# Second feed-forward pass: three fp32 down-projection tiles in place of an f16 part and a rest for two of them

## What is computed

```python
def _quantize_activations_groupwise(x):      # 5 groups of 6 images, the last 2 images give 0
    for g in range(NUM_GROUPS):
        ag = x[g * gs:(g + 1) * gs]
        gamma = jnp.max(jnp.abs(ag))
        xq = xq.at[g * gs:(g + 1) * gs].set(jnp.clip(ag * QB / (gamma + EPS), -QB + EPS, QB - EPS))
    return xq

def _bitlinear(x, W, b):
    Wb = _binarize_weights_groupwise(W)      # -1, 0 or 1
    y = jnp.einsum('btc,oc->bto', x, Wb) + b
    return _quantize_activations_groupwise(y)
h = _bitlinear(x, W1, b1)                    # 96 -> 384
h = jax.nn.gelu(h, approximate=False)
out = _bitlinear(h, W2, b2)                  # 384 -> 96
```

## Time and profile before

| | |
|---|---|
| median of 3 runs | 942.24 us (942.08 to 942.28) |
| profiled execution, first to last instruction | 940.3 us |
| TensorE busy in that span | 850.6 us, 90% |
| VectorE busy | 709.4 us, 75% |
| ScalarE busy | 473.9 us, 50% |
| GpSimd busy | 249.0 us, 26% |
| second pass | about 750 to 924 us of the span |

### The profile page before, as it was taken

One profiled execution on the slowest core, in us unless ns is written; L12 is line 12 of the kernel. 1 busy time (PEld: TensorE's weight loads), 2 busy tenths in 40 slices (PEclk: granted clock), 3 DMA queues, 4 the chain that ended last, 5 costly groups with the idle time before them and its releaser, 6 DMA issues.

```text
span 940.3 us, 18317 instructions
## 1 busy us (share of the span) xinstructions
PE 850.6 (90%) x6053; PEld 683.1 (73%) x6053; DVE 709.4 (75%) x2091; ACT 473.9 (50%) x614; POOL 249.0 (26%) x201
## 2 busy tenths in 40 slices
PE   1799929999999999999999999999999799888882
PEld 1799916788888888888888888888888655444441
DVE  4678982577777777777778777777777558999998
ACT  2244131354545454545445454545454398788981
POOL 1002610223222322322232223222322002434542
PEclk9999995899999999999999999999999999999996
DMA  9910000011001100100010001001110010363334
GB/s 214 232 35 0 1 0 14 14 30 51 26 26 38 39 26 26 51 26 26 26 51 26 26 26 51 26 26 29 47 32 20 14 39 14 103 180 97 108 103 141
DMA packets 19950, 48.35 MB, mean 51 GB/s; under 512 B 4622, under 2 KB 4818, under 8 KB 19922
## 3 DMA queue, kind: packets, MB, share of 16 engines
q1 hardware_dynamic: 17008, 46.97, 18.3%
q10 hardware_dynamic: 2914, 1.03, 0.6%
HBM read 29.33 MB, written 18.67 MB: 51 GB/s over the span
## 4 chain that ended last, share of the span: by engine, by line
PE 69%; DVE 10%; issue 8%; DMA 5%; POOL 5%; ACTq 1%; ACT 1%; SPq 0%; DVEq 0%; POOLq 0%
PE slot L799 17%; PE slot L780 10%; PE slot L709 9%; PE slot L842 8%; POOL xs L511 5%; PE slot L929 5%; PE slot L727 4%; PE slot L900 4%; DMA xs<-out 3%; PE slot L806 3%; PE slot L809 3%; PE slot L794 3%; DVE W2last L1163 2%; DMA projb<-in_L_attn_proj_b 1%; ACTq L521 1%
## 5 line engine op out<-in xcount | busy, mean ns | idle before, releaser
L799 PE MATMUL slot<-w2s,hT 128*112 128x96 f32 x1344 | 166.7, 273 | 0.0
L1234 DVE TENSOR_SCALAR xh<-t,ln_mv,ln_rs 112x96 f32<-112x96 f32 x434 | 109.3, 325 | 60.0 <-POOL ln_rs L483 60.0
L799 PEld LDWEIGHTS slot<-w2s,hT 128*112 128x112 f32 x1344 | 145.3, 181 | 11.0 <-issue 0.5
L608 ACT ACTIVATE hT<-slot,b1c,w_unit 128x784 f32<-128x784 f32 x96 | 95.9, 1005 | 105.2 <-PE slot L780 105.2
L488 POOL TENSOR_TENSOR xn_lo<-xn,xn_hi 96x784 f16<-96x784 f32 x32 | 53.4, 1670 | 272.0 <-ACT xn_hi L597 272.0
L615 ACT ACTIVATE stage<-slot,minus_one 112x768 f32<-112x768 f32 x64 | 52.5, 821 | 119.4 <-PE slot L842 119.3
L511 POOL TENSOR_TENSOR xs<-xs,xn 96x784 f32<-96x784 f32 x24 | 64.1, 2670 | 127.8 <-DVE xn L1377 93.5
L483 POOL TENSOR_TENSOR ln_rs<-ln_ve,pow_half 112x7 f32<-112x7 f32 x62 | 91.8, 1481 | 4.8
L662 ACT ACTIVATE hT<-slot,s 128x784 f32<-128x784 f32 x90 | 81.0, 926 | 20.4 <-DVE stage L1347 14.4
L806 PE MATMUL slot<-big,W1b 99*128 (+1 forms) x360 | 90.2, 331 | 0.0
L809 PE MATMUL slot<-big,W1b 96*128 (+1 forms) x360 | 89.9, 330 | 0.0
(11 more groups left out here) (178 smaller groups left out, 1504.7 us busy)
## 6 DMA issues: line engine op xcount, KB each, us to landing
big<-in_x SPq DMA_DIRECT2D x8, 1176.0 KB, 11.4
xs<-in_x SPq DMA_DIRECT2D x32, 294.0 KB, 3.1
out<-t2T SPq DMA_DIRECT2D x32, 294.0 KB, 3.3
xs<-out SPq DMA_DIRECT2D x24, 294.0 KB, 3.2
out<-xs SPq DMA_DIRECT2D x24, 294.0 KB, 2.7
big<-out SPq DMA_DIRECT2D x1, 1764.0 KB, 10.5
out<-big SPq DMA_DIRECT2D x6, 294.0 KB, 2.6
w_raw<-in_L_conv_w ACTq DMA_DIRECT2D x2, 144.0 KB
```

What stands on the lines that cost most here:

```text
L608: nc.scalar.activation(hT[:, t, :].rearrange("p (a n) -> p a n", a=2), halves((0, one, 2)[t], P), ACT.Relu, scale=w1_unit[:, t:t + 1], bia ...
L799: ins = mm(o[:, j, :], hT[:, t, j * TOK:(j + 1) * TOK], w2s[:, v, t, :], start=False, stop=t == TILES - 1, skip_group_check=True)
L1234: ins = V.tensor_scalar(dst[:, j, :], src[:, j, :], ln_mv[n][:, j, 0:1], ln_rs[n][:, j:j + 1], ALU.subtract, ALU.mult)
```

## The change

All three inner tiles are kept as clipped fp32 in `hc`, three tiles for each of two images in turn, in the memory that held the parts and rests. ScalarE's casts (`gelu_hi`) and their semaphore `hi_parts` go. VectorE's `split` becomes one clip for each tile, and takes over the wait until the buffer of two images earlier is free. `W2b` is fp32, `W2last` and its copy go, and TensorE does 6 fp32 matmuls per image in place of 8 with f16 and 2 with fp32.

```diff
-        W2b = sb("W2b", [P, TILES, C], BF16)
-        W2last = sb("W2last", [P, C])
+        W2b = sb("W2b", [P, TILES, C])
...
-        stage16 = stage[:, :].bitcast(F16)
-        SPLIT = TILES - 1
-        part = SPLIT * HW
-        per_r = 2 * part + 2 * HW
-        h_hi, h_lo = ([stage16[:, r * per_r + n * part:r * per_r + (n + 1) * part].rearrange(
-            "p (t n) -> p t n", t=SPLIT) for r in range(2)] for n in range(2))
-
-        h_last = [stage16[:, r * per_r + 2 * part:(r + 1) * per_r].bitcast(F32) for r in range(2)]
+        hc = [stage[:, r * TILES * HW:(r + 1) * TILES * HW].rearrange("p (t n) -> p t n", t=TILES) for r in range(2)]
...
-            def gelu_hi(b, t, r):
-                wait_apart(act, gelu_ready, 3 * b + t + 1, act_passed)
-                if t == 0:
-                    wait_count(act, y2_ready, b - 1)
-                    if not isinstance(b, int):
-                        act.sem_inc(act_passed, 1)
-                nc.scalar.copy(h_hi[r][:, t, :], gel[:, t, :]).then_inc(hi_parts, 1)
...
-                    gelu_hi(b, 0, r)
                     gelu_tile(g, b, 2)
-                    gelu_hi(b, 1, r)
...
-                for t in range(SPLIT):
+                for t in range(TILES):
                     pe.wait_ge(parts_ready, 3 * b + t + 1)
-                    for part, src in enumerate((h_hi[r], h_lo[r])):
-                        for h in range(2):
-                            mm(S[3][0:C, h, 0:HALF], W2b[:, t, :], src[:, t, h * HALF:(h + 1) * HALF],
-                               start=t == 0 and part == 0, stop=False, skip_group_check=True)
-                pe.wait_ge(parts_ready, 3 * b + TILES)
-                for h in range(2):
-                    ins = mm(S[3][0:C, h, 0:HALF], W2last[:, :], h_last[r][:, h * HALF:(h + 1) * HALF],
-                             start=False, stop=True, skip_group_check=True)
+                    for h in range(2):
+                        ins = mm(S[3][0:C, h, 0:HALF], W2b[:, t, :], hc[r][:, t, h * HALF:(h + 1) * HALF],
+                                 start=t == 0, stop=t == TILES - 1, skip_group_check=True)
                 ins.then_inc(y2_ready, 1)
...
-            V.tensor_copy(W2last[:, :], W2b[:, TILES - 1, :])
...
             def split(m, r):
                 b = 2 * m + r
-                for t in range(SPLIT):
-                    dve.wait_ge(hi_parts, SPLIT * b + t + 1)
-                    V.scalar_tensor_tensor(h_lo[r][:, t, :], gel[:, t, :], Q_CLIP, h_hi[r][:, t, :],
-                                           ALU.min, ALU.subtract).then_inc(parts_ready, 1)
-                dve.wait_ge(gelu_ready, 3 * b + 3)
-                V.tensor_scalar(h_last[r][:, :], gel[:, 2, :], Q_CLIP, None, ALU.min).then_inc(parts_ready, 1)
+                wait_count(dve, y2_ready, b - 1)
+                for t in range(TILES):
+                    dve.wait_ge(gelu_ready, 3 * b + t + 1)
+                    V.tensor_scalar(hc[r][:, t, :], gel[:, t, :], Q_CLIP, None, ALU.min).then_inc(parts_ready, 1)
```

More of the change, by code:

```diff
@@ L361, in build @@
         qc_ready = sem("qc_ready")
-        hi_parts = sem("hi_parts")
         o_ready = sem("o_ready")
```

## The result

The changed kernel takes 956.77 us (median of 4 runs, 955.51 to 957.44), the kernel before on the same chip 942.26 (942.08 to 943.22). The ratio is 1.0148, with a 95% interval of 1.0133 to 1.0162. It is slower by 14.5 us. The prediction was 955.1, in a range of 952.3 to 959.5. The profiled execution spans 954.8 us against 940.3.

The account below looks back on a forecast made before the run. TensorE was to become the second pass's bound at 5.97 us per image. +13.7 for the pass, -0.6 tail and -0.2 setup make +12.9 on 942.24, so 955.1 us, range 952.3 to 959.5.

Parts of the forecast that it names:

- TensorE becomes the bound: Second feed-forward pass: tiles 0 and 1 go from 0.66 to 1.32 us each, making TensorE's period 5.97 against 5.54.
- The sum of the pass: Second pass: 30 down-projections, 28 up-projections, four boundaries and holds end it at 936.9 against 923.23, +13.7 us.
- The boundaries: Four group boundaries in the second pass: TensorE's transposing and broadcasting costs 0.98 us each, 3.9 in all.
- The holds: Behind the four boundaries: VectorE's clips held by GpSimd's additions come late, 0.3 us each, 1.2 in all.
- The start: Up to the first down-projection: 0.3 us earlier as a TensorE wait goes, and 0.2 from the setup.
- The setup: Setup: removing the weight tile's copy gains only 0.2 us, as GpSimd's memset holds the next cast to 109.16 instead.
- Rival B: Setup: the cast behind the removed copy is not held, 10.9 to 12.4 us earlier, 943 to 944; chance 0.04.
- The tail: End of the pass: the last absmax no longer waits behind a held clip, 0.6 us less.
- Rival A: Later groups: VectorE's 3.82 and a GpSimd add of 2.17 bound them, 5 to 10 us more, 960 to 965; chance 0.12.
- One sign: Second pass: among the signs of a right forecast, VectorE was to idle for the GELUs; no size given.
- What bounds the kernel before: Second pass before: no engine bounds all of it; ScalarE's 5.34 us per image is nearly the period of 5.54.
- rival C: Second pass: TensorE is not the bound if an fp32 tile costs under 1.18 us; 15 saved, 927; chance 0.01.

Follow-up runs that it names:

- experiment 2: The changed kernel with ScalarE's two casts per image kept, into a spare tile that nothing reads: 956.70 us.
- experiment 5: The changed kernel without the down-projection matmuls of tile 1, its share of the result left out: 923.76 us.
- experiment 6: The changed kernel with GpSimd's addition for each finished image cut from 784 columns to 2: 955.52 us.
- Experiment 3: The kernel before with GpSimd's memset of ones moved earlier, to where GpSimd idles: 931.92 us, ratio 0.9877.
- experiment 1: The changed kernel with tile 0 back as f16 part and rest, tiles 1 and 2 clipped fp32: 945.20 us, ratio 1.0020 to the kernel before.
- experiment 12: The kernel before with the ones written early, additions on VectorE, four residual buffers instead of two and some loops written out: 911.71 us, ratio 0.9672.
- experiment 9: The changed kernel with the residual addition joined to VectorE's second clip and none on GpSimd: 955.19 us, ratio 1.0142 to the kernel before.

## Why the prediction held, point by point

**TensorE becomes the bound, and each tile costs 0.66 more.** Right, and shown from both sides: 1.68 us more of casts on ScalarE changed nothing (experiment 2), 1.32 less on TensorE changed much (experiment 5). The period was 5.95 against 5.97.

**The sum of the pass.** 180.2 was predicted and 180.7 measured, partly by luck. The boundaries cost 0.83 each and not 0.98, 0.6 less in all, and 30 down-projections of 3.95 and 28 up-projections of 2.00 are 0.6 less than counted. One term was missing. The last down-projection has no up-projection in front, so it waits for the eviction of the image before:

```profile
931.61 1.48 PE L941 MATMUL slot<-stage,W2b 128*96 128x392 f32 x4
934.26 1.23 PE L941 MATMUL slot<-stage,W2b 128*96 128x392 f32 x3 [1.17 <-ACT big L658]
```

From 931.61 + 4 x 0.33 = 932.9 to 934.26 are 1.3 us that my count of up- and down-projections doesn't contain. The holds that I put at 1.2 are 1.3 by experiment 6, and they lie where the prediction had them: the down-projection of the next image behind each of the four boundaries takes 0.13, 0.35, 0.34 and 0.42 longer than 3.95, and in experiment 6 it does not.

**The start.** The time from the span's start to the first down-projection was predicted 0.5 shorter (0.3 for a wait, 0.2 in the setup) and came 0.6 longer. With the 0.5 of the pass this makes up, to a tenth, the 1.6 between 953.2 and the span of 954.8. The 0.3 was too much in any case: the 0.40 in the earlier trace rows is idle time of the weight loads, and the matmul in question started 0.17 late, at 756.31 instead of 755.81 + 0.33. That wait did go. That only 0.6 separate the two starts is luck. In the kernel before and in the changed one:

```profile
130.00:200.00 70.00, 61.05 (x371) 45.94 (x370) 36.40 (x136) 24.40 (x32) 11.74 (x11) 0.78 0.06 18
...
726.00:757.00 31.00, 25.86 (x181) 20.90 (x180) 14.81 (x41) 12.07 (x19) 1.68 (x2) 0.89 0.08 21
...
734.11 1.52 PE L929 MATMUL slot<-R,xh1T 97*112 97x96 f32 x14
```

```profile
130.00:200.00 70.00, 60.87 (x406) 47.67 (x403) 38.94 (x151) 26.42 (x34) 13.44 (x13) 0.85 0.06 18
...
729.94 1.52 PE L910 MATMUL slot<-R,xh1T 97*112 97x96 f32 x14
```

The changed kernel began the first pass 0.3 later (142.49 against 142.19). At its beginning it had the higher granted clock, 0.85 against 0.78, and at the same matmuls near its end it was 4.2 ahead, 729.94 against 734.11. From there to the first down-projection it had the lower clock (0.68 from 726 to 757.6, last section) and took 27.7 where the kernel before took 22.9. Two differences of 4.5 and 4.8 us, neither of them a term of mine, nearly cancelled.

**The setup.** Right in its mechanism: the hold moved to the next cast, to 109.55. The 0.2 us of gain don't show at the start of the first pass. Rival B's price was right too. Experiment 3 frees the setup by taking away the memset instead of the copy, and gains 11.3, against 10.9 to 12.4.

**The tail.** The last absmax follows its eviction at once, 939.52 after 938.58 + 0.91, and the tail is 0.5 shorter; 0.6 was predicted.

**Rival A** is out as the bound of the later groups: in the changed kernel, the boundaries aside, all their images but one of each group take 5.95 to 6.03. That one takes 6.08 to 6.37, and in experiment 5 it still takes 6.0, with TensorE's work cut to 4.63: there the rival's reckoning is close.

**One sign did not come.** VectorE was to idle for the GELUs. In the pass it waits 2.9 us for them, and 32.3 us for the evictions ahead of its absmax.

**What bounds the kernel before: this reading was wrong, though the sum didn't rest on it.** I gave ScalarE 5.34 us per image from the durations of its records. They overlap. In the timeline of the kernel before, at a busy place:

```profile
773.73 0.96 ACT L662 ACTIVATE hT<-slot,s 128x784 f32<-128x784 f32 x1
774.54 0.89 ACT L671 CAST stage<-hT 128x784 f16<-128x784 f32 x1
775.27 0.96 ACT L675 ACTIVATE big<-slot,fb2c 96x784 f32 x1
776.08 1.76 ACT L662 ACTIVATE hT<-slot,s 128x784 f32<-128x784 f32 x2
```

From start to start a GELU and an eviction cost 0.81, a cast 0.73: 4 x 0.81 + 2 x 0.73 = 4.70 per image. The first group of the kernel before, in which GpSimd adds nothing, already runs at this pace:

```profile
771.67 1.52 PE L961 MATMUL slot<-stage,W2b 128*96 128x392 f16 x8
...
776.37 1.52 PE L961 MATMUL slot<-stage,W2b 128*96 128x392 f16 x8
```

So ScalarE, 27.66 of 28.00 busy, or TensorE with its 4.65 bounds there, and neither explains 5.54. Most of what made 5.54 of it was the hold of VectorE by GpSimd, worth 21.0 us of the pass. The same mistake stands in rival C: a TensorE need below 5.54 was not enough to win, as experiment 1 showed with 5.29.

So the change did remove a stall of some 21 us, but with more work of TensorE, 39.6, in its place: 166.2 - 21.0 + 39.6 = 184.8 would be the sum if no other slack took part, and 180.7 was measured. Where hardly anybody else is in the way (experiment 12's form against experiment 9's), three fp32 tiles cost 179.4 - 148.0 = 31.4 us more in the pass.

## What to carry to other kernels

A change that relieves two engines and loads the third is settled by the third's start-to-start times alone, if these come out above the present period. Before one acts on a period that no engine's work explains, look for clips and casts from SBUF to SBUF on VectorE with durations several times their median, and see what GpSimd does beside them: here one such addition per image and one memset in the setup cost 21 and 11 us, and joining the addition to a VectorE instruction, moving the memset, and loading further ahead took 31 us off the kernel before, to which the change added 14.5. And what an instruction is held by matters more than its length: the weight tile's copy, 15.69 us long, was removed, and the next cast took its place.

## What the runs showed of the hardware

A GpSimd addition of 1.84 us alone is recorded with up to 3.89 where VectorE's instructions on two SBUF inputs run beside it, and VectorE's clip of 0.56 with 2.1 to 2.25 where the addition came first. That the one which comes later waits to the end fits the Trainium skill, page "SBUF — State Buffer", section "Who interferes with whom". Not every clip beside an addition's record was held: in the timeline of the kernel before one ran in its usual 0.56. Counted back from the end of the addition's record, 844.63 + 3.89 = 848.52, its own 1.84 begin at 846.68, about where that clip ends (846.80). So the addition was presumably still waiting; this is a reckoning and not a measurement.

```profile
844.47 1.85 DVE L1347 SCALAR_TENSOR_TENSOR stage<-hT,stage 128x784 f16<-128x784 f32 x2
844.63 3.89 POOL L511 TENSOR_TENSOR xs<-xs,xn 96x784 f32<-96x784 f32 x1 [1.10 <-DVE xn L1377]
...
846.24 0.56 DVE L1350 TENSOR_SCALAR stage<-hT 128x784 f32<-128x784 f32 x1
```

The stretch ahead of the second pass, in which TensorE waits often, has another granted clock from execution to execution. The stretch view from 726 to the first down matmul, of the changed kernel and of experiment 2:

```profile
726.00:757.60 31.60, 26.66 (x147) 21.21 (x146) 12.79 (x36) 9.93 (x16) 1.68 (x2) 0.68 0.07 20
```

```profile
726.00:750.60 24.60, 18.69 (x146) 14.78 (x146) 12.56 (x36) 10.45 (x17) 1.68 (x2) 1.00 0.08 25
```

Nearly the same work took 31.6 us at a mean of 0.68, much of it at the lower of the two levels (1.2 and 2.4 GHz), and 24.6 at 1.00. These 7.0 us are the difference between the spans of the two profiled executions, 954.8 and 947.9. Experiment 2's runs go from 949.8 to 959.1. That the clock made this spread too is not shown, as only one of them was profiled, and the mean clock listed for the run of 956.70 (0.983) is above that of the run of 949.78 (0.980). Comparisons of a few us on this kernel need either the pass alone or many runs. Why one execution keeps the clock there and another doesn't was not settled.
